# Wider x rows over five stages, with four of the 24 t summed on Pool

## What is computed

```python
# x: (B=1024, T=24, S=1024)   W1: (S, T)   b1: (S,)   W2: (S, S)   b2: (S,)
h = sigmoid(einsum('bts,st->bs', x, W1) + b1)
y = h @ W2.T + b2
```

## Time and profile before

| what | value |
|---|---|
| median of 3 runs | 347.9 us (347.64 to 350.02) |
| span of the profiled execution | 348.0 us |
| mean granted TensorE clock | 0.960 of full speed |
| PE, PEld busy | 86%, 73% |
| DVE busy | 83% |
| ACT, POOL busy | 24%, 35% |
| HBM read, written | 104.96 MB, 4.19 MB |

### The profile page before, as it was taken

One profiled execution on the slowest core, in us unless ns is written; L12 is line 12 of the kernel. 1 busy time (PEld: TensorE's weight loads), 2 busy tenths in 40 slices (PEclk: granted clock), 3 DMA queues, 4 the chain that ended last, 5 costly groups with the idle time before them and its releaser, 6 DMA issues.

```text
span 348.0 us, 6554 instructions
## 1 busy us (share of the span) xinstructions
PE 299.0 (86%) x1989; PEld 254.0 (73%) x1989; DVE 287.4 (83%) x425; ACT 82.0 (24%) x137; POOL 123.2 (35%) x104
## 2 busy tenths in 40 slices
PE   4874978899999999999899969978979969799686
PEld 3663967799889877888788857757857757587564
DVE  2757798999899989998989887765978969789696
ACT  1122363221311131114021212221412413124140
POOL 0000000555344252423324324441744726547270
PEclk9889699999999999999999999996989999989999
DMA  8999999999999999999999999999999999999906
GB/s 242 383 351 383 348 349 349 348 351 348 349 349 348 348 348 348 348 348 348 348 348 348 307 284 309 337 320 281 288 273 286 291 288 288 274 277 296 290 14 241
DMA packets 143253, 109.41 MB, mean 314 GB/s; under 512 B 5497, under 2 KB 140673, under 8 KB 143234
## 3 DMA queue, kind: packets, MB, share of 16 engines
q1 hardware_dynamic: 141600, 106.97, 103.4%
q10 hardware_dynamic: 1634, 2.20, 1.8%
HBM read 104.96 MB, written 4.19 MB: 314 GB/s over the span
## 4 chain that ended last, share of the span: by engine, by line
PE 32%; SPq 30%; DMA 26%; issue 6%; DVE 5%; ACT 1%; DVEq 0%; ACTq 0%
SPq L155 29%; DMA ring<-in_r_x 26%; PE bank L197 19%; PE bank L221 12%; DVE acc L311 3%; DVE acc L334 1%; PE bank L212 1%; DVE acc L307 0%; ACT h L391 0%; SPq L163 0%; ACT L391 0%; DVE w_lo L322 0%; DVE acc_odd L311 0%; DVE y L366 0%; SPq L166 0%
## 5 line engine op out<-in xcount | busy, mean ns | idle before, releaser
L197 PE MATMUL bank<-ident,ring 128*128 128x128 f32 x1536 | 210.4, 286 | 39.6 <-DMA ring<-in_r_x 35.8
L311 DVE SCALAR_TENSOR_TENSOR acc<-bank,w,acc 128x512 f32<-128x512 f32 x296 | 205.6, 744 | 37.4 <-PE bank L197 36.4
L197 PEld LDWEIGHTS bank<-ident,ring 128*128 128x128 f32 x1536 | 181.4, 147 | 70.6 <-DMA ring<-in_r_x 42.6
L462 POOL TENSOR_TENSOR y<-stage,y 128x512 f32<-128x512 f32 x78 | 99.8, 1281 | 146.6 <-ACT stage L401 146.5
L401 ACT COPY stage<-bank 128x512 f32<-128x512 f32 x78 | 45.7, 586 | 208.0 <-PE bank L221 200.1
L221 PE MATMUL bank<-w_hi,h_hi 128*128 (+1 forms) x128 | 57.4, 448 | 1.6 <-DVE h_lo L358 1.6
L311 DVE SCALAR_TENSOR_TENSOR acc_odd<-bank,w,acc_odd 128x512 f32<-128x512 f32 x66 | 49.1, 744 | 8.0 <-PE bank L197 7.5
L221 PE MATMUL bank<-w_hi,h_lo 128*128 (+1 forms) x128 | 50.7, 396 | 0.0
L221 PE MATMUL bank<-w_lo,h_hi 128*128 (+1 forms) x128 | 50.3, 393 | 0.0
L452 POOL TENSOR_TENSOR h_lo<-h,h_hi 128x512 fp32r<-128x512 f32 x15 | 18.9, 1276 | 67.0 <-ACT h_hi L396 67.0
L221 PEld LDWEIGHTS bank<-w_hi,h_lo 128*128 128x128 f32 x128 | 24.2, 189 | 5.6
(11 more groups left out here) (20 smaller groups left out, 23.0 us busy)
## 6 DMA issues: line engine op xcount, KB each, us to landing
ring<-in_r_x SPq DMA_DIRECT2D x120, 512.0 KB, 8.7
ring<-in_r_x SPq DMA_DIRECT2D x144, 256.0 KB, 5.3
y<-in_L_rec_W SPq DMA_DIRECT2D x2, 2048.0 KB, 13.1
out_y<-y ACTq DMA_DIRECT2D x4, 512.0 KB, 5.5
out_y<-y SPq DMA_DIRECT2D x8, 256.0 KB, 2.3
w<-in_L_rec_W ACTq DMA_DIRECT2D x1, 96.0 KB, 4.5
b1row<-in_L_rec_b ACTq DMA_DIRECT2D x1, 4.0 KB
b2row<-in_L_rec_b ACTq DMA_DIRECT2D x1, 4.0 KB
```

The costliest lines, as they stand in the source:

```text
L197: mm = pe.transpose(bank[u % XBANKS][:, j * P:(j + 1) * P], ring[:, r % RING, j, col:col + P], ident[:, :])
L311: nc.vector.scalar_tensor_tensor(out=to, in0=bank[u % XBANKS][:, :], scalar=wcol, in1=to, op0=ALU.mult, op1=ALU.add).then_inc(unit_added, 1)
L462: nc.gpsimd.tensor_tensor(piece, stage[:, (at + k) % STAGES, :], piece, ALU.add).then_inc(y_written, 1)
```

## The change

- **Stages.** Five stages take the place of the eight blocks: (group, first chunk, chunks) = (0, 0, 4), (0, 4, 4), (1, 0, 3), (1, 3, 3), (1, 6, 2). A load is one t of a stage in one DMA: rows of 2 KB (1 MB), 1.5 KB (768 KB) or 1 KB (512 KB). `ring` has six slots of one t.
- **Four t on Pool.** t = 0 to 3 (`NK`) go, at the places (3, 11, 15, 19) or (1, 6, 11, 16) of a stage's 24 loads, not to `ring` but to `nat`, which has two slots. Pool multiplies them in their own layout by a row of W1 that is spread over the partitions (`w1all`) and sums them in `nsum`: one multiplication for the first t, a multiplication and an addition for each of the other three. PE turns `nsum` once for each chunk, ahead of the last two t, and DVE adds it without a weight. A stage has 21 units for a chunk, 336 in all.
- **w1all** is made in stage 0: 32 transposes of broadcast columns of W1, eight copies on ACT.
- **Products** are summed over all chunks of a stage in one PSUM bank: 12, 12, 9, 9 and 6 matmuls for each of the eight outputs, 384 in all as before. They are spread evenly over the units of the next stage from the tenth on (`steps_due`). Of stages 0 and 2, ACT copies the sum from PSUM to `y`; Pool adds b2 to it (`add_b2`, four operations of 128x1024 for each group, placed after the `low_parts` of stages 1 and 3); of stages 1 and 3, DVE adds the sum from PSUM to `y` (`add_out`). The adds through `stage`, the 78 on Pool among them, are gone, and so are `acc_odd` and the merges. `y` has room for one group.
- **Tail.** The last stage has two chunks after the last unit: 48 matmuls. The first chunk's h is split in pieces, the second's in one.
- **W2** is loaded into `h`, `nat[1]` and `y`; the second load to `nat` waits until eight of its 16 pieces are turned. b2 is spread by a DMA with a partition broadcast.

```diff
+NK = 4
+STAGES = (
+    (0, 0, 4, (3, 11, 15, 19)),
+    (0, 4, 4, (1, 6, 11, 16)),
+    (1, 0, 3, (1, 6, 11, 16)),
+    (1, 3, 3, (1, 6, 11, 16)),
+    (1, 6, 2, (1, 6, 11, 16)),
+)
-    CW = 2
-    RING = 4
+    RING = 6
+    NATS = 2
...
+        order = [("x", t, c) for t in ts[:-2] for c in range(n)]
+        order += [("n", 0, c) for c in range(n)]
+        order += [("x", t, c) for t in ts[-2:] for c in range(n)]
...
+        def steps_due(i, v):
+            lead, rest = 10, 3
+            span = len(units[i]) - lead - rest
+            return max(0, min(product_steps(i), -(-(v - lead + 1) * product_steps(i) // span)))
...
         def _(sp):
+            for i, (g, c0, n, places) in enumerate(STAGES):
+                for at in range(T):
...
+                    if at in places:
+                        if m == 1:
+                            sp.wait_ge(w2_turned, SC)
+                        if m >= NATS:
+                            sp.wait_ge(nat_freed, m - NATS + 1)
+                        sp.dma_start(nat[:, m % NATS, :, :n * P], x_v[g, :, :, t, cols]).then_inc(nat_loaded[m % NATS], 16)
+                        m += 1
+                    else:
+                        q = item_of[i, t]
+                        if q >= RING:
+                            sp.wait_ge(unit_turned, item_end[q - RING] + 1)
+                        sp.dma_start(ring[:, q % RING, :, :n * P], x_v[g, :, :, t, cols]).then_inc(x_loaded[q % RING], 16)
...
         def _(pe):
+            def product_step(b, k):
...
+                    if n == 0:
+                        pe.wait_ge(h_hi_ready, first_h[b] + nch)
+                    if n >= 2 and b % 2 == 0:
+                        pe.wait_ge(part_kept, b // 2 * OUTS + n - 1)
+                    if n >= 2 and b % 2 == 1:
+                        pe.wait_ge(y_added, b // 2 * OUTS + n - 1)
...
+                if n == 0 and r == 2 * nch:
+                    pe.wait_ge(h_lo_ready, first_h[b] + nch)
...
         def _(dve):
+                if kind == "n":
+                    nc.vector.tensor_tensor(acc[:, c, :], xbank[u % XBANKS][:, :], acc[:, c, :], ALU.add).then_inc(unit_added, 1)
...
         def _(act):
+                if i < LAST:
+                    act.wait_ge(out_summed, OUTS * i)
+                    for c in range(chunks[i]):
+                        act.wait_ge(h_ready, first_h[i] + c + 1)
+                        nc.scalar.copy(h_hi[:, c, :], h[:, c, :]).then_inc(h_hi_ready, 1)
...
         def _(pool):
+                for k in range(NK):
+                    m = i * NK + k
+                    row = w1all[:, k, c0 * P:(c0 + n) * P].unsqueeze(1).to_broadcast([P, JT, n * P])
+                    slot = nat[:, m % NATS, :, :n * P]
+                    pool.wait_ge(nat_loaded[m % NATS], 16 * (m // NATS + 1))
+                    if k == 0:
...
+                        nc.gpsimd.tensor_tensor(ssum, slot, row, ALU.mult).then_inc(nat_freed, 1)
+                    else:
+                        nc.gpsimd.tensor_tensor(slot, slot, row, ALU.mult).then_inc(nat_weighed, 1)
...
+                        nc.gpsimd.tensor_tensor(ssum, ssum, slot, ALU.add).then_inc(nat_freed, 1)
...
+            for i in range(NS):
+                weighted_sum(i)
+                if i < LAST:
+                    low_parts(i)
+                if i in (1, 3):
+                    add_b2(i // 2)
```

More of the change, by code:

```diff
@@ L182, in _, with turn_unit @@
         def _(pe):
[L183 to L201, removed]
+            def turn_unit(i, v):
+                u = first_unit[i] + v
+                kind, t, c = units[i][v]
+                if u >= XBANKS:
+                    pe.wait_ge(unit_added, u + 1 - XBANKS)
+                if kind == "x":
+                    q = item_of[i, t]
+                    if c == 0:
+                        pe.wait_ge(x_loaded[q % RING], 16 * (q // RING + 1))
+                    tile = ring[:, q % RING, :, c * P:(c + 1) * P]
+                else:
+                    if c == 0:
+                        pe.wait_ge(nat_freed, NK * (i + 1))
+                    tile = nsum[:, :, c * P:(c + 1) * P]
+                for j in range(JT):
+                    mm = pe.transpose(xbank[u % XBANKS][:, j * P:(j + 1) * P], tile[:, j, :], ident[:, :])
+                mm.then_inc(unit_turned, 1)
@@ L326, in _ @@
-            spread = {W2_AT + W2_EVERY * m + 2: lambda m=m: split_w2(m) for m in range(OH * SC)}
-            for r in range(SLOTS):
-                add_slot(0, r, first=True, between=spread)
-            with dve.Fori(1, APART) as i:
-                for r in range(SLOTS):
-                    add_slot(i, r)
-            def merge(c, rows=slice(0, BANK)):
-                nc.vector.tensor_tensor(acc[:, c, rows], acc[:, c, rows], acc_odd[:, rows],
-                                        ALU.add).then_inc(merged, 1)
@@ new lines, in _ @@
+            for c in range(chunks[LAST]):
+                pieces = [slice(j * P, (j + 1) * P) for j in range(JT)] if c == 0 else [slice(0, BANK)]
+                for k, rows in enumerate(pieces):
+                    at = c and JT + c - 1 or k
+                    dve.wait_ge(h_ready, first_h[LAST] + at + 1)
+                    nc.vector.tensor_copy(h_hi[:, c, rows], h[:, c, rows]).then_inc(tail_hi, 1)
+                    dve.wait_ge(tail_hi, at + 1)
+                    nc.vector.tensor_tensor(h_lo[:, c, rows], h[:, c, rows], h_hi[:, c, rows].bitcast(F32),
+                                            ALU.subtract).then_inc(tail_lo, 1)
@@ new lines, in low_parts, with add_b2 @@
+            def low_parts(i):
+                for c in range(chunks[i]):
+                    pool.wait_ge(h_hi_ready, first_h[i] + c + 1)
+                    nc.gpsimd.tensor_tensor(h_lo[:, c, :], h[:, c, :], h_hi[:, c, :].bitcast(F32),
+                                            ALU.subtract).then_inc(h_lo_ready, 1)
+            def add_b2(g):
+                pool.wait_ge(b2_loaded, 16)
+                pool.wait_ge(part_kept, (g + 1) * OUTS)
+                for j in range(JT):
+                    nc.gpsimd.tensor_tensor(y[:, j, :], y[:, j, :], b2all[:, :], ALU.add).then_inc(b2_added, 1)
```

497 lines of the change are left out of this document (218 added, 279 removed).

## The result

The changed kernel takes 337.1 us (median of 4 runs, 336.1 to 337.9) against 349.0 us for the kernel before beside it. The ratio is 0.966, with a 95% interval of 0.962 to 0.971: 11.8 us faster. The forecast was 321 us, so the direction was right and the gain less than half of the one expected. The time lies in the range of 310 to 339. It is also the 337 us of rivals 2 and 3, so the time alone would not tell the cases apart; the profile does.

A forecast was written before the change was run, and what follows sets the result against it. DMA time was taken as the bound; of 42 us saved, 9 go to gaps and 7 to PE. Stream end 297, last unit 304, plus tail 17.8, is 322, less 1 for rounding: 321 us; range 310 to 339.

The forecast's parts named there:

- rival 2: Loads of x: 2 KB and 1.5 KB rows run no faster than about 350 GB/s; 337 us, chance 0.14.
- Rival 3 (the clock): PE falls to the lower clock after each load to nat, 1.2 us each in stages 1 to 4; 337 us, chance 0.09.
- The rates of long rows: Loads of x: 385 GB/s for 2 KB rows and 370 for 1.5 KB; the stream could end at 288.8 us.
- The line through the 512 B and 1 KB rows: DMA time per row, 9.9 ns plus 18.6 for each 512 B: 389 GB/s for 2 KB, 374 for 1.5 KB.
- Pool's prices: Pool's two-input operations take 2.30 ns per column: 4.8, 3.6 and 2.5 us for 2048, 1536 and 1024 columns.
- f: Factor on Pool's weighted_sum for the unproven spread operand; at 1, seven operations take 33.6 us in a four-chunk stage.
- rival 4: Pool's chain of low parts, add_b2 and weighted_sum becomes the bound; 348 us at f = 1.5; chance 0.08.
- The holes: Load stream stops while SP waits: gaps of about 2 us in stage 0, 2 in stage 2, 5 in stage 4.
- such a case: Within the main case: gaps in stages 2 and 4 each 4 us longer, kernel at 330 us.
- PE starts products when h_hi is there (93.5) and needs 74 x 4 x 0.109 + 22.2 more: 148: Stage 1: PE starts products at 93.5 us and, after its remaining transposes and matmuls, ends at 148.
- PE last in stage 4: End of stage 4: PE turns the last unit at 304 us, 7 us after the stream's end at 297.
- The tail: After the last unit: DVE's last operations 2.8, 48 matmuls 11.5, last add and store 3.5; together 17.8 us.

The follow-up runs named there:

- experiment 5: Changed kernel with each load of stages 0 and 1 cut into two DMAs of 1 KB rows: 349.2 us, ratio 1.001 to the kernel before.
- experiment 6: Control: changed kernel with the loads of stages 0 and 1 cut by rows into two 512 KB DMAs keeping 2 KB rows: 337.2 us, ratio 0.967.
- experiment 8: Changed kernel with Pool's four loads at later places, 5, 9, 13, 17 in stage 1, and so in stages 2 to 4: 327.1 us, ratio 0.937.
- experiment 7: Changed kernel with the matmuls ending 20, 12 and 12 units before the end of stages 1, 2 and 3, in place of 3: 336.2 us, ratio 0.962.
- experiment 3: Changed kernel with all 24 t through PE and DVE, no loads to nat, no weighted sum on Pool, b2 still on Pool: 321.0 us, ratio 0.920.

## Why the prediction was right or wrong

**The rates of long rows: right.** 385 and 370 GB/s were taken, 387 and 373 came. Without its holes the stream would have ended at 308.8 - 21.3 = 287.5 us; the sum said 288.8. The line through the 512 B and 1 KB rows (389 and 374 for 2 and 1.5 KB) held. Rival 2 (capped rates) is out, and experiments 5 and 6 show that it is the row and not the DMA. The two figures of the Trainium skill (DMA: Bandwidth & Descriptors, Specifications) did not hold here: rows of 512 B ran at 287 GB/s and not at line rate, and 387 GB/s were sustained above the 358. The table works that figure out as a stack's 716 GB/s divided by two cores; this kernel used one core, and whether the other was at work no run here shows.

**Pool's prices: right.** The groups by shape (mean ns in the last column before the idle time):

```profile
L451 POOL TENSOR_TENSOR nsum<-nsum,nat 128x2048 f32<-128x2048 f32 x6 | 27.4, 4572 | 0.5
L448 POOL TENSOR_TENSOR nat<-nat,w1all 128x1536 f32<-128x1536 f32 x6 | 20.8, 3465 | 7.7 <-DMA nat<-in_r_x 7.7
L463 POOL TENSOR_TENSOR y<-y,b2all 128x1024 f32<-128x1024 f32 x8 | 18.8, 2381 | 0.0
```

4.57, 3.47 and 2.38 us against 4.8, 3.6 and 2.5; f is 0.95, and rival 4 is out. The spread operand costs nothing: the two multiplications with it into `nsum` at 2048 columns (L446) took 4574 ns, the additions without it 4572. The Trainium skill (GPSIMD Engine Reference, the table at N = 2048), at 4.5 us, was nearer than my line from the earlier trace rows, and this trace agrees with it.

**The holes: right in their places and causes, wrong in size.** This is the step that failed: the times at which the chains of low parts, `add_b2` and first piece were to end. In them above all the end of stage 1 on PE, put at 148 us and measured at 158, was wrong: it had PE's waits for x at nothing and started from a stage 0 taken 5 us too short. All three came where the text has them, but with 4.4, 6.8 and 10.1 us in place of 2, 2 and 5. The 12.3 us between 21.3 and 9 are the 12 us by which the stream ends late (308.8 for 297), and they reach the last unit whole (317.7 for 304). Of the 15.1 us between the sum of 321 and the span of 336.1, the stream's end is 11.8, PE's lag behind it 1.9, the tail 0.6 and the rounding that was taken off 0.8. The text had priced such a case, at 330 with the gaps in stages 2 and 4 each 4 us longer; they were 4.8 and 5.1 longer, and that in stage 0 2.4. The times of the chain, predicted and measured:

| step | predicted | measured |
|---|---|---|
| W2's eighth piece turned | 43.5 | 47.2 |
| DVE ends stage 0 | 88 | 93.7 |
| low parts of stage 1 begin, end | 151.4, 156.5 | 161.1, 166.0 |
| first piece free in stage 2 | 169.9 | 178.9 |
| low parts of stage 3 begin, end | 258.9, 262.8 | 272.3, 276.0 |
| first piece free in stage 4 | 275.1 | 287.8 |
| stream ends | 297 | 308.8 |
| last unit turned | 304 | 317.7 |

From the end of the low parts to the free piece the interval was right: 12.9 us measured for 13.4 predicted in stage 2, 11.8 for 12.3 in stage 4. Late was the start of that chain, by 9.7 us in stage 2 (start, length, engine in the timeline of the changed kernel, and PE's waits for x from 112 to 160 us):

```profile
31.98 2.79 PE L207 MATMUL xbank<-ident,ring 128*128 128x128 f32 x12 [6.30 <-DMA ring<-in_r_x]
98.53 0.48 PE L267 MATMUL pbank<-w_hi,h_hi 128*128 128x512 f32 x1
108.10 0.63 PE L207 MATMUL xbank<-ident,ring 128*128 128x128 f32 x4 [1.86 <-DMA ring<-in_r_x]
161.05 5.00 POOL L456 TENSOR_TENSOR h_lo<-h,h_hi 128x512 fp32r<-128x512 f32 x4 [19.44 <-ACT h_hi L421]
```

```profile
PE xbank L207 <- DMA ring<-in_r_x: 2.6, 2, 1.5
```

About 5 us come from stage 0. The sum let DVE set the pace there without a pause; in fact PE waits 6.3 us for x, until 32 us, while W2's loads pass, and DVE waits with it, so that W2's eighth piece is turned 3.7 us late. After the hole DVE waits another 4.7 us before the stage ends.

Nearly as much comes from the step "PE starts products when h_hi is there (93.5) and needs 74 x 4 x 0.109 + 22.2 more: 148". The first matmul of the product comes at 98.5, five microseconds late for what went wrong in stage 0. To its 54.5 us of work belong 4.5 us of waits for x (1.9 at 108 us, 2.6 after 112), which the step has at nothing. Together that gives 157.5, and PE turned the stage's last unit at about 158. That the loads for Pool, which lie between those for PE, make these waits fits the order of the loads, but no run tests it: with those loads at later places (experiment 8) stage 1 ended only 0.7 us sooner.

By the bytes of the slices, the stream ended stage 0 at 84 us and stage 1 at 149; DVE ended them at 93.7 and 159.7. PE and DVE thus stayed 10 us behind the stream, although their sums for the stage are 6 and 9 us shorter than its 65. A sum smaller than the bound's does not mean that an engine catches up. My first reason for the lag, the even spread of the matmuls, was tested by experiment 7 and is wrong; what keeps the lag at 10 us stays open.

What SP waits is the chain's end less the time at which load 10 has landed and nothing is left to move. In stage 4 the chain ends 12.7 us late, the stream runs dry 7.1 late (279.2 for 272.1, the two holes before it), and the hole is 5.1 longer. In stage 2 the chain ends 9.0 us late, the stream of x runs dry about 3 late, and the first stores of group 0 fill part of the rest (127 GB/s from 176 to 178 us): the hole is 4.8 longer. So lateness that costs nothing on PE costs in full on SP, as far as the stream is not late itself. I had treated each hole as small because both times came out nearly equal (169.9 and 169.8), and did not carry a few us of error in either as a risk of the same size. The experiments on the cause agree from three sides: take the additions away (17.7 us), move the waiting place by two loads (10 us), or let nothing wait (16 us, experiment 3).

**PE last in stage 4: right.** The last unit is turned 8.9 us after the stream's end (7 predicted).

**The tail: right within 1 us.** 336.1 - 317.7 = 18.4 for 17.8. The chain of waits, start and length:

```profile
320.01 2.14 PE pbank L301 x6
322.15 5.25 PE xbank L301 x18
327.39 1.36 PE pbank L301 x6
328.75 4.09 PE xbank L301 x18
332.87 0.69 DVE y L365
```

The second 24 matmuls take 5.45 us as expected, the first 7.39.

**Rival 3 (the clock)** did not decide anything in stage 1, where it was priced first: from 84 to 149 us the granted clock is 1.00 throughout. In stage 0 something like it is there. Behind the loads to `nat` PE waits 2.9 to 3.0 us for x three times, before 55, 67 and 78 us, and the windows that follow have 0.60, 0.80 and 0.58. Low stretches also lie behind the second and third hole (0.50 from 184 to 190 and from 292 to 296 us) where PE works off what had waited; what they cost was not separated. The mean is 0.934 for 0.960.

**Readings that were wrong without changing the sum.** The DMA share of the earlier trace rows is at 9 up to the third last slice, not the second last. The 0.50 at 236 to 240 us of the earlier trace rows stands behind waits for x of 2.0 and 0.9 us, not of 3 us and more. Twice the price of rival 3 gives 353 us or more, which is over 1% above the kernel before. And 321 is a span: in all these runs the time is 1.7 to 2.8 us above it (337.88 for 336.1), so that the forecast of a time should have been about 323, and the nearness of the span of 348.0 to the median before means little (one of the three runs took 350.0).

## What to carry to other kernels

When work is moved to an idle engine, look at who waits for it in the queue that feeds the bound: 18.8 us of additions on a half-idle Pool cost 17.7 us, because the one queue that issues the loads waited for what came behind them. Place a load that must wait for a slow consumer as late in the queue as its data allow; a further slot for it should help too, but was not tried here. And cost a hole from the lateness of its chain, not from mean times: PE and DVE, shorter by sum, stayed 10 us behind the stream at the end of both four-chunk stages.

## What the runs showed of the hardware that was not expected

The load of W1 (96 KB in 96 B rows, issued on ACT's queue at 0.74 us in both kernels) took 4.5 us to land before and 9.7 after; DVE's first operation waits for it until 10.5 us. The DMA issues of the kernel before and of the changed kernel:

```profile
w<-in_L_rec_W ACTq DMA_DIRECT2D x1, 96.0 KB, 4.5
```

```profile
w<-in_L_rec_W ACTq DMA_DIRECT2D x1, 96.0 KB, 9.7
```

It is not the length of SP's rows that goes with it: the control of experiment 6, with 2 KB rows in DMAs of 512 KB, has 4.4 us, and experiment 5, with 1 KB rows in DMAs of 512 KB, 5.0. All kernels whose first loads of x are DMAs of 1 MB have 9.3 us or more. At the end it costs nothing that shows, since the control takes as long as the changed kernel.

In the tail PE stood still for 2.3 us ahead of the first matmul, and the first 24 ran at 0.308 us each against 0.227 for the next 24; the granted clock over the window from 318 us to the end is 0.91. In shorter windows it is 0.88 from 318 to 322 us, 0.80 from 322 to 328, where the first 24 run, and 1.00 from 328 to 333, so most of the 1.9 us between them goes with the clock.
